# A new prologue for a fused attention and expert kernel: loads under four semaphores, a second row buffer, score weights made in halves

## What is computed

```python
x = x + _layernorm(_L0_attn_ref(_layernorm(x), key_param, Wq, bq, Wk, bk, Wv, bv, Wo, bo))
x = x + _layernorm(_L0_ffn_ref(_layernorm(x), slot_query, d_Wq, ..., c_Wq, ..., e_W1, e_Wg, e_W2, ...))

# _L0_attn_ref: 16 heads of 16, against 32 learned pattern rows, with sparsemax for softmax
queries = (query @ Wq + bq); keys_flat = k @ Wk + bk; values = keys_flat @ Wv + bv
A = sparsemax(scale * einsum('blhe,bshe->bhls', queries, keys))
out = einsum('bhls,bshd->blhd', A, values) @ Wo + bo
# _L0_ffn_ref: 16 slots gather from x by attention (d_*), pass one gated expert each
# (e_W1, e_Wg, e_W2 of 256 x 1024), and x reads them back by attention (c_*)
```

## Time and profile before

| | |
|---|---|
| median of three executions | 473.92 us |
| the profiled execution | 473.89 us |
| its span, first to last instruction | 472.2 us |
| what lies around the span | 1.7 us |
| VectorE, ScalarE, GpSimd busy | 313.0, 226.1, 149.4 us |
| TensorE busy (matmuls) | 395.3 us |
| mean granted clock of TensorE | 0.954 |
| memory traffic | 83.78 MB, 177 GB/s over the span |

### The profile page before, as it was taken

How to read it: one execution, slowest core, us unless ns; L and a number is a source line. 1 busy time by engine, 2 the same in 40 slices (tenths; PEclk the granted TensorE clock), 3 DMA queues, 4 the chain that set the end, 5 groups by cost and what they waited for, 6 DMA issues and landing times. The chain is left out here.

```text
span 472.2 us, 6963 instructions
## 1 busy us (share of the span) xinstructions
PE 395.3 (84%) x2085; PEld 245.2 (52%) x2091; DVE 313.0 (66%) x1189; ACT 226.1 (48%) x412; POOL 149.4 (32%) x243
## 2 busy tenths in 40 slices
PE   3886576778977988899999899989998379999983
PEld 3542232234544444565766675734444137888872
DVE  3699999986999998477415245243333124989996
ACT  2235558565685889677773744200000001356671
POOL 4104735655567453333032010010000000335353
PEclk9997988788999999899999999999999989999997
DMA  4384111010101054637717867759999999901215
GB/s 149 90 279 128 40 45 29 16 44 2 44 1 46 1 168 165 228 114 243 269 70 289 310 191 285 258 208 393 400 385 403 383 383 337 341 1 46 73 62 178
DMA packets 44319, 83.78 MB, mean 177 GB/s; under 512 B 1911, under 2 KB 36349, under 8 KB 39933
## 3 DMA queue, kind: packets, MB, share of 16 engines
q1 hardware_dynamic: 43224, 82.15, 49.5%
q10 hardware_dynamic: 1060, 1.22, 0.9%
HBM read 70.78 MB, written 12.58 MB: 177 GB/s over the span
## 5 line engine op out<-in xcount | busy, mean ns | idle before, releaser
L1087 PE MATMUL bank<-Wz,yT 128*128 128x512 f32 x128 | 70.8, 705 | 25.9 <-DVE top L1666 23.3
L1087 PEld LDWEIGHTS bank<-Wz,yT 128*128 128x128 f32 x128 | 28.0, 227 | 61.6 <-issue 50.4
L1666 DVE MAX8 top<-bank 128x8 f32<-128x32 f32 x512 | 51.5, 179 | 1.9 <-ACT arena L762 1.7
L1023 ACT ACTIVATE d<-d 128x32 f32<-128x32 f32 x16 | 3.7, 229 | 86.9 <-DVE d L2045 86.9
L595 POOL TENSOR_SCALAR veps<-mv 128x4 f32<-128x4 f32 x24 | 5.9, 246 | 99.8 <-DVE mv L1594 71.7
L703 POOL TENSOR_TENSOR work<-work 128x512 f32<-128x512 f32 x16 | 16.6, 1061 | 64.8 <-DVE work L2120 64.8
L1120 PE MATMUL bank<-aWo,hoT 128*128 128x256 f32 x128 | 36.0, 404 | 0.1
L1154 PE MATMUL bank<-arena,Wd 128*128 128x512 f32 x64 | 29.3, 600 | 3.8 <-ACT arena L825 3.8
L1183 PE MATMUL bank<-d,work 128*128 128x256 f32 x128 | 30.3, 382 | 1.9 <-ACT d L853 1.9
L1526 PE MATMUL bank<-scr,work 128*128 128x256 f32 x128 | 29.1, 381 | 1.6 <-ACT work L1036 1.6
L1502 PE MATMUL bank<-scr,arena 128*128 128x256 f32 x128 | 28.9, 380 | 0.0
(11 more groups left out here) (272 smaller groups left out, 881.4 us busy)
## 6 DMA issues: line engine op xcount, KB each, us to landing
arena<-in_L_ffn_e_W_dram SPq DMA_DIRECT2D x14, 1024.0 KB, 11.0
scr<-in_L_ffn_e_W_dram SPq DMA_DIRECT2D x7, 1024.0 KB, 13.5
x<-in_L_ffn_e_W_dram SPq DMA_DIRECT2D x5, 1024.0 KB, 4.8
x<-in_L_ffn_e_Wg_dram SPq DMA_DIRECT2D x5, 1024.0 KB, 10.2
xin<-in_L_attn_query_dram SPq DMA_DIRECT2D x8, 512.0 KB, 4.0
x<-in_L_attn_query_dram SPq DMA_DIRECT2D x1, 4096.0 KB, 16.6
out_dram<-x SPq DMA_DIRECT2D x8, 512.0 KB, 5.4
away_dram<-arena SPq DMA_DIRECT2D x8, 512.0 KB, 8.6
```

The source lines that it names most:

```text
L1087: mm = pe.matmul(bZ[t % 2][:, :], yT[:, c, t * P:(t + 1) * P], Wz[:, c, :], start=(c == 0), stop=(c == C - 1))
L1666: mx = v.max(top[:, h * TG + t, :], bZ[t % 2][:, h * NS:(h + 1) * NS])
```

## The change

It touches the prologue alone, apart from the place of one copy.

- Loads. `w_in` becomes four semaphores: `k_in` (patterns and the biases bq, bk), `wq_in`, `wk_in`, and `w_in` for the rest. SyncE issues group 0's rows, aWq, aWk, then group 1's rows into a place of their own (`xin1`, in the buffer `d` that is first used by the threshold), then the five weights of `w_in1`; group 2's rows wait only for group 0's to be normalized, and the load of x follows them. ScalarE issues all fourteen small loads at the start and none later.
- The biases lie in two tiles (`browA` with the first two, `browB` with seven), so that they can be turned in two steps; `miscT` is copied in two pieces.
- TensorE turns patterns and `browA`, waits for aWq, and so on; it makes half 0 of `Wz`, turns group 0's rows, and makes half 1. VectorE copies half 0, ScalarE half 1. The scores of tiles 2 and 3 of group 0 and `turn_y(1)` come ahead of the second layer's dWq and aWv products; the first scores of group 1 come ahead of the `Wd` product.
- ScalarE normalizes three tiles of group 1, copies the scores of tile 0, normalizes the fourth, and goes on.
- VectorE takes group 1's statistics before it copies half 0 of `Wz`; `sel32` and `sel` come after. `fold_dispatch` is cut in two: its part on the keys stays between the sorts of tiles 1 and 2, its part on the queries comes after the first threshold; `keep_dispatch` comes after the first sorts of group 1.
- GpSimd waits for group 0's normalization before it writes group 1's scale and shift; VectorE waits for GpSimd's `rst[0]` before group 1's statistics.

```diff
-        brow = fold(2464, P, 18)
+        browA = fold(2464, P, 4)
+        browB = fold(3744, P, 14)
...
+        xin1 = d[:, 0:1024].rearrange("p (t d) -> p t d", t=TG)
...
-        (M_MISC, M_AQ, M_KQ, M_WZ, M_DK, M_DQ, M_V, M_WD) = range(1, 9)
+        (M_KP, M_AQ, M_KQ, M_MISC, M_WZ, M_DK, M_DQ, M_V, M_WD) = range(1, 10)
...
-        first_by_sync = [weight(aWk, 'L0_attn_Wk', "(p c) n -> p c n", w_in), weight(aWq, 'L0_attn_Wq', "(p c) n -> p c n", w_in),
-                         (kp, A['L0_attn_key_param'][0], w_in)] + biases(rows_of[:6])
-        first_by_scalar = [(sq[:, :], A['L0_ffn_slot_query'][0], w_in), (b2, A['L0_ffn_e_b2'], w_in)] + biases(rows_of[6:]) + [
-            (bo3, A['L0_attn_bo'].rearrange("(o d) -> o d", o=1).broadcast_to([3, D]), bo_in),
-            (cbo[:, :], A['L0_ffn_c_bo'].rearrange("(o d) -> o d", o=1).broadcast_to([P, D]), bo_in)] + [
+        first_by_sync = [weight(aWq, 'L0_attn_Wq', "(p c) n -> p c n", wq_in), weight(aWk, 'L0_attn_Wk', "(p c) n -> p c n", wk_in)]
+        second_by_sync = [
             weight(dWk, 'L0_ffn_d_Wk', "(p c) n -> p c n", w_in1), weight(dWq, 'L0_ffn_d_Wq', "(p c) n -> p c n", w_in1),
             (bvrow, A['L0_attn_bv'].rearrange("(o d) -> o d", o=1), w_in1),
             weight(aWv, 'L0_attn_Wv', "(c p) n -> p c n", w_in1), weight(aWo[:, :, :], 'L0_attn_Wo', "(c p) n -> p c n", w_in1)]
-        N_W0, N_W1 = (sum(s is which for _, _, s in first_by_sync + first_by_scalar) for which in (w_in, w_in1))
+        first_by_scalar = [(kp, A['L0_attn_key_param'][0], k_in)] + biases(rows_of[:2]) + [
+            (sq[:, :], A['L0_ffn_slot_query'][0], w_in), (b2, A['L0_ffn_e_b2'], w_in)] + biases(rows_of[2:]) + [
+            (bo3, A['L0_attn_bo'].rearrange("(o d) -> o d", o=1).broadcast_to([3, D]), bo_in),
+            (cbo[:, :], A['L0_ffn_c_bo'].rearrange("(o d) -> o d", o=1).broadcast_to([P, D]), bo_in)]
+        N_K, N_W0, N_W1 = (sum(s is which for _, _, s in first_by_sync + second_by_sync + first_by_scalar)
+                           for which in (k_in, w_in, w_in1))
...
-            next_load(1, 0)
-            next_load(2, 0)
+            sp.dma_start(xin1, xs[:, 0, TG:2 * TG, :]).then_inc(xin1_in, 16)
+            for dst, src, s in second_by_sync:
+                sp.dma_start(dst, src).then_inc(s, 16)
+            sp.wait_ge(y_ready, TG)
+            load(2, 0)
             sp.dma_start(x[:, :, :], xt).then_inc(x_in, 16)
             next_load(3, 0)
...
             roots(0, 0)
+            hold(y_ready, TG)
...
-            for dst, src, s in first_by_scalar[:-5]:
+            for dst, src, s in first_by_scalar:
...
             norm_y(0, guard=False)
-            for dst, src, s in first_by_scalar[-5:]:
-                act.dma_start(dst, src).then_inc(s, 16)
             put_yT(0, guard=False)
-            norm_y(1)
-            put_scores(0, 0, range(TG))
+            act.wait_ge(wz_ps, 1)
+            act.activation(Wz[:, 1, :], bZ[1][:, :], ACT.Copy).then_inc(wz_sb, 1)
+            norm_y(1, tiles=range(3))
+            put_scores(0, 0, range(1))
+            norm_y(1, tiles=range(3, TG))
+            put_scores(0, 0, range(1, TG))
             put_yT(1)
             put_scores(1, 0, range(2))
...
-            pe.wait_ge(w_in, 16 * N_W0)
+            pe.wait_ge(k_in, 16 * N_K)
             for c in range(C):
                 pe.transpose(bank[7][:, c * NS:(c + 1) * NS], kp[:, c::C], ident[0:NS, 0:NS])
-                pe.transpose(bank[7][:, 64 + c * NE:64 + (c + 1) * NE], sq[:, c::C], ident[0:NE, 0:NE])
-                pe.transpose(bank[7][:, 96 + c * NE:96 + (c + 1) * NE], b2[:, c::C], ident[0:NE, 0:NE])
-            pe.transpose(bank[7][:, 128:146], brow, ident[0:18, 0:18]).then_inc(pe_part, 1)
+            pe.transpose(bank[7][:, 64:68], browA, ident[0:4, 0:4]).then_inc(pe_part, 1)
...
+            pe.wait_ge(wq_in, 16)
             turn_weight(aWq, 5)
-            pe.wait_ge(dve_part, M_MISC)
+            pe.wait_ge(dve_part, M_KP)
+            pe.wait_ge(wk_in, 16)
             for m in range(2):
                 for c in range(C):
                     mm = pe.matmul(bank[4][:, m * NS:(m + 1) * NS], aWk[:, c, m * P:(m + 1) * P], kpT[:, c, :],
                                    start=(c == 0), stop=(c == 1))
             mm.then_inc(pe_part, 1)
-            turn_y(0)
-            pe.wait_ge(dve_part, M_KQ)
+            pe.wait_ge(w_in, 16 * N_W0)
+            pe.transpose(bank[6][:, 0:14], browB, ident[0:14, 0:14])
             for c in range(C):
+                pe.transpose(bank[6][:, 14 + c * NE:14 + (c + 1) * NE], sq[:, c::C], ident[0:NE, 0:NE])
+                mm = pe.transpose(bank[6][:, 46 + c * NE:46 + (c + 1) * NE], b2[:, c::C], ident[0:NE, 0:NE])
+            mm.then_inc(pe_part, 1)
+            def fold_scores(c):
                 for m in range(2):
                     mm = pe.matmul(bZ[c][:, m * 256:(m + 1) * 256], aWqT[:, m, c, :], bdK[:, m, :, :],
                                    start=True, stop=True)
-            mm.then_inc(pe_part, 1)
+                return mm
+            pe.wait_ge(dve_part, M_KQ)
+            fold_scores(0).then_inc(pe_part, 1)
+            turn_y(0)
+            fold_scores(1).then_inc(wz_ps, 1)
             pe.wait_ge(dve_part, M_WZ)
+            pe.wait_ge(wz_sb, 1)
             scores_of(0, range(2))
             pe.wait_ge(w_in1, 16 * N_W1)
             turn_weight(dWk, 5)
+            scores_of(0, range(2, TG))
+            turn_y(1)
...
-            turn_y(1)
-            scores_of(0, range(2, TG))
+            scores_of(1, range(2))
...
-            scores_of(1, range(2))
...
-            own(v.tensor_reduce(sel32[:, :], ident[:, :].rearrange("p (k x) -> p x k", x=32), AX_X, ALU.add))
-            own(v.tensor_reduce(sel[:, :], ident[:, :].rearrange("p (h e) -> p e h", e=NE), AX_X, ALU.add))
-            v.wait_ge(pe_part, M_MISC)
-            v.tensor_copy(miscT[:, :], bank[7][:, 0:146]).then_inc(dve_part, 1)
+            v.wait_ge(pe_part, M_KP)
+            v.tensor_copy(miscT[:, 0:68], bank[7][:, 0:68]).then_inc(dve_part, 1)
...
+            v.wait_ge(pe_part, M_MISC)
+            v.tensor_copy(miscT[:, 68:146], bank[6][:, 0:78]).then_inc(dve_part, 1)
...
+            v.wait_ge(rst[0], 1)
+            first_statistics(1)
             v.wait_ge(pe_part, M_WZ)
-            own(v.tensor_copy(Wz[:, 0, :], bZ[0][:, :]), wait=False)
-            v.tensor_copy(Wz[:, 1, :], bZ[1][:, :]).then_inc(dve_part, 1)
-            def fold_dispatch():
+            v.tensor_copy(Wz[:, 0, :], bZ[0][:, :]).then_inc(dve_part, 1)
+            own(v.tensor_reduce(sel32[:, :], ident[:, :].rearrange("p (k x) -> p x k", x=32), AX_X, ALU.add), wait=False)
+            own(v.tensor_reduce(sel[:, :], ident[:, :].rearrange("p (h e) -> p e h", e=NE), AX_X, ALU.add), wait=False)
+            def fold_dispatch_keys():
                 v.wait_ge(pe_part, M_DK)
+                v.wait_ge(dve_part, M_WZ)
                 raised(1, dWkT, bank[5][:, :], DBK, lambda r_: r_.then_inc(dve_part, 1))
+            def fold_dispatch_queries():
...
-            first_statistics(1)
             v.wait_ge(bo_in, 32)
             own(split3(ab3[:, :], bo3))
             sort_top(0, range(2))
-            fold_dispatch()
+            fold_dispatch_keys()
             sort_top(0, range(2, TG))
             threshold(0)
-            keep_dispatch()
+            fold_dispatch_queries()
             def batch_of_scores(i, b):
                 first_statistics(i + 2)
                 sort_top(i + 1, range(2))
+                if isinstance(i, int) and i == 0:
+                    keep_dispatch()
...
```

More of the change, by code:

```diff
@@ L113, in build @@
         kpT = miscT[:, 0:64].rearrange("p (c s) -> p c s", c=C)
-        sqT = miscT[:, 64:96].rearrange("p (c s) -> p c s", c=C)
-        b2T = miscT[:, 96:128].rearrange("p (c s) -> p c s", c=C)
-        bcol = miscT[:, 128:146].rearrange("p (v m) -> p v m", m=2)
+        bcol = miscT[:, 64:82].rearrange("p (v m) -> p v m", m=2)
+        sqT = miscT[:, 82:114].rearrange("p (c s) -> p c s", c=C)
+        b2T = miscT[:, 114:146].rearrange("p (c s) -> p c s", c=C)
         ABQ, ABK, ABV, DBQ, DBK, DBV, CBQ, CBK, CBV = range(9)
@@ L230, in build @@
         w_in1 = sem("w_in1")
+        k_in = sem("k_in")
+        wq_in = sem("wq_in")
+        wk_in = sem("wk_in")
+        xin1_in = sem("xin1_in")
+        wz_ps = sem("wz_ps")
+        wz_sb = sem("wz_sb")
         bo_in = sem("bo_in")
@@ L353, in biases @@
         def biases(names):
-            return [(brow[2 * v:2 * v + 2, :], A[name].rearrange("(m p) -> m p", p=P), w_in) for v, name in names]
+            return [(browA[2 * v:2 * v + 2, :] if v < 2 else browB[2 * v - 4:2 * v - 2, :],
+                     A[name].rearrange("(m p) -> m p", p=P), k_in if v < 2 else w_in) for v, name in names]
         def weight(w, name, form, s):
@@ L748, in norm_y @@
                 for t in tiles:
-                    scaled(0, t, y[:, t, :], xin[:, t, :]).then_inc(y_ready, 1)
```

(16 more changed lines are left out.)

## The result

The changed kernel takes **471.5 us** (median of 15 executions, 470.08 to 472.5), the kernel before beside it 473.73 (15 executions). The ratio is 0.9959, with a 95% interval of 0.9944 to 0.9974: faster by 1.9 us, between 1.2 and 2.7. The forecast was 4.7 us. The profiled execution of after took 472.26 us, of which 470.5 are its span.

The account below looks back on a forecast made before the run. VectorE was taken to bound the loop, which starts with the first sorts. The sort coming 4.9 us earlier, less 0.25, gave 4.7 us: 467.5 + 1.7 = 469.2 us (chance 0.70), range 467.2 to 471.8.

Parts of the forecast that it names:

- The sum up to the sort: Prologue: earlier loads and reordered work bring the first sort from 24.52 to 19.6 us, 4.9 us earlier.
- the rival of the late small loads: Prologue: small loads served behind SyncE's queue land at 12.3, fold starts at 12.9, gain 2.4 us, 471.5 us; chance 0.10.
- From the sort to the loop: First sort to first count: VectorE's 17.5 us of work is only permuted; waiting for tile 1 costs 0.25 us.
- tile 1's 0.25: After the first sort: VectorE waits 0.25 us because tile 1's scores and copy take longer than the sorting.
- a gain before 105 us reaches the end: Loop and experts: the expert stream starts when computation says so, so the prologue's 4.7 us gain carries through.
- the stream of the experts: Rival, experts: if their weights paced from earlier than read, nothing comes out, 473.9 us; chance 0.05.
- the empty stretch: Before the experts: queues move 1 GB/s for three us; forecast to remain, 4.7 us earlier.
- half lost in the loop: Rival, loop: shifted clock dips add stalls, losing 1 to 2 us, 471 us; chance 0.05.
- The clock: Rival, first four tiles: TensorE's clock stays low, each tile costs 3.4 us, +1.4 us, 475.3 us; chance 0.05.

Follow-up runs that it names:

- e1: The changed kernel with the queries' part of the second layer's fold put back ahead of the first threshold; -6.7 us against before (-8.1 to -5.4).
- e2: The changed kernel with each half of bdQ made by one instruction reading PSUM, without the copy dQT; -6.7 us against before (-8.1 to -5.3).
- e8: The changed kernel with the queries' part moved further back, amid GpSimd's subtractions, bdQ made with one operand from PSUM; 469.5 us, -4.9 against before.
- e9: The changed kernel with the queries' part moved further back, amid GpSimd's subtractions, products with both operands in SBUF; 470.1 us, -3.4 against before.
- e3: The kernel before with only the changed order after the first sorts (queries, Wd's copy, group 1's scores); +3.2 us against before (+2.1 to +4.4).
- e4: e1 with turn_y(0) ahead of both fold halves and group 1 normalized whole before any score copy; -5.1 us against before (-7.1 to -3.0).
- e0: The changed kernel once more, unchanged; -2.1 us against before (-3.0 to -1.1).
- e5: e1 with TensorE waiting at its start for all the first loads, as for one semaphore; -0.9 us against before (-2.0 to +0.3).
- e6: e1 with group 1's rows loaded into the one buffer xin once group 0 is normalized; -2.4 us against before (-3.8 to -1.0).
- e7: e2 with 14 matmuls without use ahead of the loop's second scores, to keep TensorE's clock up; -4.4 us against before (-5.7 to -3.1).

## Why the prediction was wrong

**The sum up to the sort held.** `miscT` 7.16 (forecast 6.9), `bdK` done 10.70 (10.6), first score matmul 17.20 (16.85), first sort 19.87 (19.6), and 18.79 in a second profile of the same kernel. Such closeness is partly luck: the two profiles are 1.1 us apart, mostly because half 1 of the fold took 1.91 us in one and 1.03 in the other, where the clock was up sooner. Inside the sum, two terms were off. `xin` was seen at 5.35, not 4.97. And the last small load was seen at 10.30, not 8.5: issued at 4.95, so 5.35 us and not the 3.9 of the earlier trace rows, while the queues moved 365 GB/s at a DMA share of 1.03. (The prediction also says that all first loads had arrived by 6 to 7 us in before; its own has the last one at 8.08.) TensorE stood idle for 0.97 us of that wait, and the fold's start at 10.97 was at most 0.3 late. So the rival of the late small loads was half right in its premise and wrong in its price. That its 471.5 us is the time that was measured is chance.

**The step that failed** is "From the sort to the loop": "From 24.52 to the first `count` at 42.05 VectorE does 17.5 us of work without a gap, and the change only permutes it". It is a permutation of instructions, not of durations. What a step costs depends on what runs on GpSimd beside it: line 1615 cost 0.49 us ahead of the threshold and 3.92 behind it. I costed the moved queries at their old row, and never asked what ran beside them in the new place, although the same paragraph says that GpSimd's first subtraction follows the threshold there. The account for after: forecast of `count` 37.3; 0.3 for the later sort, 3.43 for the products, nothing for tile 1's 0.25, makes 40.8, and 41.01 was measured. Three kernels remove the hold-up in two ways (another place in `e1`, one operand in PSUM in `e2` and `e8`), `e9` halves it, and `e3` makes it in the kernel before.

**It could be read in before.** The trace that the prediction was made from has the same hold-up in another instruction of two SBUF operands, the running sum of line 1673. It takes 1.22 us where GpSimd is idle and 1.58 where it begins 0.50 us ahead of the end of GpSimd's line 617:

```profile
33.96 1.22 DVE L1673 TENSOR_TENSOR_SCAN top<-chain,top 128x512 f32<-128x512 bf16 x1
...
50.73 1.58 DVE L1673 TENSOR_TENSOR_SCAN top<-chain,top 128x512 f32<-128x512 bf16 x1
```
```profile
47.59 3.64 POOL L617 TENSOR_TENSOR arena<-arena,tauf 128x2048 f32 x1 [4.89 <-DVE tauf L1721]
```

All seven later ones of before are held up so, and end 1.08 us after GpSimd's instruction. This also answers in part whether `e2` and `e8` escaped by their kind of instruction: the hold-up isn't peculiar to `tensor_tensor`. Whether a `scalar_tensor_tensor` with both operands in SBUF is held up beside a long instruction of GpSimd's, no run shows.

The Trainium skill states the rule, in "SBUF — State Buffer" (Who interferes with whom): VectorE and GpSimd share one pair of ports, an instruction of VectorE with two SBUF inputs contends with a GpSimd instruction that reads SBUF, and the second to come waits for the whole instruction. The runs agree in the number of hold-ups (two in after, one in `e9`, none with PSUM as one source) and in that the batch statistics, with one input in SBUF, take 1.39 us beside the subtraction (`e2` at 30.82, before at 37.14) as without it. They don't agree for GpSimd's power of 128x4 numbers, which reads SBUF too: in after two instructions with both tensor operands in SBUF begin inside it, at 460.74 and 461.14, and take 479 ns each, as the others of their line do (GpSimd's spans in the profile are rough, but this one has 0.98 us left at 460.74).

```profile
L2191 DVE SCALAR_TENSOR_TENSOR arena<-arena,rstd,x x12: 452/480/486, 460.0 to 467.4; 128x256 f32<-128x256 f32 x12
```
```profile
460.60 1.12 POOL L734 TENSOR_TENSOR rstd<-veps,mhalf 128x4 f32<-128x4 f32 x1
```

So what GpSimd's instruction is counts as well. By the rule two subtractions of 1.91 us would have stood in place of 0.49, an estimated loss of 3.3 us, and 4.7 less that is 1.4, near the 1.0 measured at `count`.

**What lies behind `count`.** The prediction took it that a gain before 105 us reaches the end. Over the twelve rows of the table the time against before follows `count` with a slope of 1.04 (a least-squares line through the table; correlation 0.96), each within 2 us of the shift of its own `count`, and the root mean square around the line is 0.8 us. So the time does follow `count`, and the stream of the experts doesn't keep the time: the empty stretch stands before the experts in after too, 3 us earlier, at 2 GB/s. What remains is scatter of single profiles, at two places. At the loop's end VectorE waits for TensorE either 1.32 us (after, e2, e3, e4) or 2.7 to 3.1 (before, e0, e1, e5 to e9). The first row is that of after, the second that of before:

```profile
105.28 0.15 DVE L1809 TENSOR_REDUCE flagi<-bank 1x1 int32<-1x4 f32 x1 [1.32 <-PE bank L1247]
```
```profile
108.46 0.15 DVE L1769 TENSOR_REDUCE flagi<-bank 1x1 int32<-1x4 f32 x1 [3.01 <-PE bank L1229]
```

In the eight profiles with the long wait TensorE was at the lower clock until 3.7 to 4.6 us ahead of that row, in the four with the short one it had been at the higher for 8.9 us or more. That fits the clock as the cause of these 1.7 us. The two rows stand 3.2 us apart where `count` is only 1.0 apart, and half of that goes back by the end, in the experts: VectorE's instructions start 3.39 us earlier in after up to 360 us (357.36 for 360.75) and 1.63 us earlier behind them (398.24 for 399.87). Why is open. There TensorE works at the lower clock for 10.2 us in after, in two stretches, and for 3.4 in before (us, busy us, granted clock, DMA share, GB/s of TensorE alone; after's longer stretch, then before's):

```profile
382.00:389.00 7.00, 6.89 (x41) 0.52 1.07 373
```
```profile
377.80:380.80 3.00, 3.00 (x18) 0.50 1.04 418
```

But `e4` and `e9` spend 13.7 us of the same stage at the lower clock and lose nothing there against before, so the time at the lower clock doesn't explain the loss by itself.

The rival "half lost in the loop" (1 to 2 us) thus has the right size for a single profile, but either sign. With such scatter one execution of a kernel says little: the profiled one of `e1` took 471.1 us, 4.4 above its median.

**The clock**, the rival of the other sign, didn't come in after: the first tiles took 3.67 us for two. `e6` shows that its premise was sound, after 3.09 us without work.

**The range** left out the possibility that a moved step changes its price, and so ended at 467.2 to 471.8 with 0.90 for faster. The sign was right, and the median lies just within by the range's width: the gain was 1.9 us and not 4.7.

**Open**: `e1` and `e2` gained 6.7 us where their `count` is 4.8 and 5.7 earlier, `e8` 4.9 where it is 5.5 earlier. Of the intervals those of after, `e1` and `e6` miss the shift of `count` by 0.2 to 0.5 us, but after and `e0`, the same kernel, differ by 1.1 us in `count` themselves, so no further cause is needed, and none is shown. The best kernels of the study are `e1` and `e2`, at 466.8 and 466.5 us, 1.4% under before.

## What to carry to other kernels

When a step is moved, cost it again in its new place: look in the trace at what the other engines do there, above all whether GpSimd and a VectorE instruction with two SBUF operands meet. Where they must meet, read one operand from PSUM, or place the step where GpSimd waits. Look also for a step whose price already differs between its places in the trace at hand, as the running sum's does here. And of a gain that depends on several waits (here separate semaphores and a second buffer) most is lost if one of them stays.

## What the runs showed of the hardware

- A VectorE product of 128x128 f32 with both operands in SBUF took 0.29 us alone and 1.99 to 2.00 us beside a 1.91 us subtraction of GpSimd's (128x1024), in seven of the eight cases that began inside one, ending 0.15 us after it; the eighth, in `e9`, began 0.09 us ahead of its end and took 0.29. Made by another instruction with one operand in PSUM it took 0.32 to 0.34 us in such a place (`e8`).
- A running sum of 128x512 with both operands in SBUF took 1.22 us alone and ended 1.08 us after the GpSimd instruction inside which it began, seven times in before and seven in after.
- Beside GpSimd's power of 128x4 numbers VectorE's instructions with two SBUF operands kept their durations (479 ns of 128x256 in after). So not every GpSimd instruction that reads SBUF holds them up.
- Where the product began 0.05 us ahead of GpSimd's subtraction (`e9`), the subtraction took 2.01 us instead of 1.91.
- MAX8 from PSUM, batch statistics and copies from PSUM kept their durations beside the same subtraction.
- The last small load on ScalarE's queue, issued at 4.95 to 5.22 us, was seen 4.4 to 5.4 us later in the ten profiles of the new prologue, in after while the queues moved 365 GB/s; 3.9 us later in before, on SyncE's queue behind the weights and at 176 GB/s.
- With the same TensorE work until then, TensorE's clock was granted its higher level between 13.6 and 17.0 us in eight profiles: half 1 of the fold took 1.91 us in after, `e1`, `e7` and `e9` and 1.03 to 1.05 in `e0`, `e2` and `e6`. The clock fell after some of TensorE's waits of 2.1 to 4.5 us, not after all (`e2`: after 2.15 us at 34.39, not after 2.85 at 43.56).
